# One group of small matmuls per pair of attention blocks instead of two: V of the 16 keys beyond 128, made for both blocks at once

## The reference

```python
win = xh.reshape(B, H // WS, WS, W // WS, WS, C).transpose(0, 1, 3, 2, 4, 5).reshape(-1, L, C)
qkv = (win @ qkv_w.T + qkv_b).reshape(-1, L, 3, HEADS, HD).transpose(2, 0, 3, 1, 4)
attn = jnp.einsum('bhld,bhmd->bhlm', q, k) * SCALE
attn = jax.nn.softmax(attn + bias[None], axis=-1)
out = jnp.einsum('bhlm,bhmd->bhld', attn, v).transpose(0, 2, 1, 3).reshape(-1, L, C)
out = out @ proj_w.T + proj_b
```

## Time and profile before

| | |
|---|---|
| median of 3 runs | 8950.28 us (8947.58 to 8953.78) |
| the profiled execution | 8950.57 us |
| its span | 8949.0 us |
| TensorE matmul busy (PE) | 8138.8 us, 91% |
| TensorE weight load busy (PEld) | 6102.6 us, 68% |
| VectorE (DVE), ScalarE (ACT), GpSimd (POOL) busy | 61%, 57%, 29% |
| mean granted clock of TensorE | 0.934 of full |

### The profile page before, as it was taken

How to read it: one execution, slowest core, us unless ns; L and a number is a source line. 1 busy time by engine, 2 the same in 40 slices (tenths; PEclk the granted TensorE clock), 3 DMA queues, 4 the chain that set the end, 5 groups by cost and what they waited for, 6 DMA issues and landing times.

```text
span 8949.0 us, 261096 instructions
## 1 busy us (share of the span) xinstructions
PE 8138.8 (91%) x88874; PEld 6102.6 (68%) x88874; DVE 5502.8 (61%) x20355; ACT 5135.3 (57%) x16576; POOL 2579.1 (29%) x3417
## 2 busy tenths in 40 slices
PE   9998999999999999999999999999999999999930
PEld 8996666866676667666686667666766667666720
DVE  4554777467845775377746784477637774678410
ACT  5554765466644664376546674466537653666434
POOL 1111333133322333133323332133313331334200
PEclk9998998999989998899999998999999999999865
DMA  7561000200012000200020000200020002000089
GB/s 125 97 110 35 15 21 21 82 12 21 15 32 69 21 21 15 86 15 21 22 76 18 21 15 24 77 21 21 15 86 15 21 22 84 10 21 15 23 329 410
DMA packets 386935, 487.38 MB, mean 54 GB/s; under 512 B 249617, under 2 KB 352529, under 8 KB 369297
## 3 DMA queue, kind: packets, MB, share of 16 engines
q1 hardware_dynamic: 369488, 393.67, 15.4%
q0 software_dynamic: 16192, 77.49, 2.2%
HBM read 319.45 MB, written 151.66 MB: 53 GB/s over the span
## 4 chain that ended last, share of the span: by engine, by line
PE 76%; issue 14%; DMA 4%; POOL 3%; DVE 2%; ACT 1%; POOLq 1%; SPq 0%; DVEq 0%; ACTq 0%
PE ps L946 66%; PE ps L1084 5%; POOL work L467 3%; DMA AH<-y_scratch 2%; PE ps L1129 2%; PE ps L1081 2%; DMA out<-AH 1%; PE ps L1082 1%; DVE work L801 1%; POOLq L464 0%; DVE work L765 0%; DVE work L811 0%; ACT AH L656 0%; ACT work L555 0%; POOL work L425 0%
## 5 line engine op out<-in xcount | busy, mean ns | idle before, releaser
L555 ACT ACTIVATE work<-work 128x144 f32<-128x144 f32 x5120 | 2042.8, 403 | 36.1 <-issue 35.1
L946 PE MATMUL ps<-work 128*32 128x144 f32 (+4 forms) x32902 | 1758.8, 302 | 160.0 <-issue 96.1
L765 DVE CUSTOM_DVE_ANT_0 work<-ps,negbias 128x144 f32<-128x144 f32 x5120 | 1247.1, 302 | 628.1 <-issue 435.2
L801 DVE SCALAR_TENSOR_TENSOR work<-xs,lw,work 128x570 f32<-128x570 f32 (+1 forms) x2048 | 1587.2, 812 | 0.0
L946 PEld LDWEIGHTS ps<-work 128*32 128x32 f32 (+3 forms) x32902 | 1009.9, 127 | 699.3 <-issue 563.1
L433 POOL TENSOR_TENSOR work<-work 128x80 f32<-128x80 f32 x1024 | 482.7, 471 | 3301.8 <-DVE work L772 3301.8
L946 PE MATMUL ps<-work,wqkv 128*128 128x288 f32 x4096 | 1319.4, 447 | 98.1 <-POOL work L448 78.9
L436 POOL TENSOR_TENSOR work<-work 128x640 f32<-128x640 f32 x1024 | 1309.1, 1278 | 0.0
L946 PEld LDWEIGHTS ps<-work,wqkv 128*128 128x128 f32 x4096 | 734.2, 197 | 382.9 <-POOL work L425 83.3
L555 ACT ACTIVATION_READ_ACCUMULATOR work<-work 128x1 f32 x5120 | 971.0, 190 | 0.0
L946 PE MATMUL ps<-wproj,work 128*96 128x256 f32 x3072 | 825.7, 393 | 0.0
(11 more groups left out here) (126 smaller groups left out, 11588.2 us busy)
## 6 DMA issues: line engine op xcount, KB each, us to landing
work<-in_x SPq DMA_DIRECT2D x128, 576.0 KB, 5.5
xs<-in_x SPq DMA_DIRECT2D x64, 1152.0 KB, 5.3
AH<-in_x SPq DMA_DIRECT2D x192, 384.0 KB, 3.4
y_scratch<-AH SPq DMA_DIRECT2D x192, 384.0 KB, 2.6
AH<-y_scratch SPq DMA_DIRECT2D x64, 1152.0 KB, 24.0
out<-AH POOLq DMA_DIRECT2D x64, 1152.0 KB, 17.0
xs<-in_x SPq DMA_DIRECT2D x112, 96.0 KB, 5.1
bias_scratch<-in_rpb_rev POOLq DMA_DIRECT2D x144, 4.5 KB, 2.1
```

Source lines behind the costliest of these rows:

```text
L555: o = act.activation(sp[t % 4][:, c, :], sp[t % 4][:, c, :], ACT.Exp, scale=-1.0, bias=mn[t % 4][:, c:c + 1], accum_out=den[t % 4][:, c:c ...
L765: v.tensor_tensor_reduce(out=sp[t % 4][:, c, :], in0=psS[c], in1=negbias[:, t % 2, c, :], scale=1.0, scalar=BIG, op0=ALU.add, op1=ALU.min, ...
L801: v.scalar_tensor_tensor(dst[:, ct, :, w0:w1], xs[side][:, ct, y0 + dy:y0 + dy + HS, w0 + dx - 1:w1 + dx - 1], lw[:, ct, tap:tap + 1], dst ...
L946: return nc.tensor.matmul(o, l, r, start=start, stop=stop)
```

## The change

Piece 5 loses its small matmuls. Piece 4's small matmuls take a stationary operand of 32 columns of x that holds the 16 pixels of block 0 and the 16 of block 1 (`xr`), which POOL copies together after the windows, behind a wait for its own window copies. V of the 16 keys then lies at partitions 32j to 32j+15 for block 0 and 32j+16 to 32j+31 for block 1, in one buffer for both blocks. `attend_few` contracts over all 32 rows; `normalise` writes the 16 keys' probabilities to columns 0 to 15 of `rest` for block 0 and to 16 to 31 for block 1, and the others stay zero from the memset at the head of an image (a buffer of `rest` always serves the same v). ScalarE's copy of piece 5 has 256 columns instead of 320. `xw_ready` is counted twice per pair.

```diff
-        v_sb = [carve("a", 2, C + CT * HD) for _ in range(2)]
+        xr = [carve("a", CT, 2, 16) for _ in range(2)]
+        v_sb = [carve("a", 2 * C + CT * HD) for _ in range(2)]
...
-                wait_apart(sy, (S["xw_ready"], n * NP - NP), (S["lpe_step"], n * 36 - 36))
+                wait_apart(sy, (S["xw_ready"], (n * NP - NP) * 2), (S["lpe_step"], n * 36 - 36))
...
                         last.then_inc(S["xw_ready"], 1)
+                        wait_apart(g, (S["xw_ready"], (n * NP + p) * 2 + 1))
+                        g.tensor_copy(xr[p % 2], xw[p % 2].rearrange("p t (v l) -> p t v l", v=2)[:, :, :, 0:16]
+                                      ).then_inc(S["xw_ready"], 1)
 
                     def normalise(t):
                         g.wait_ge(S["rden_ready"], n * NT + t + 1)
-                        g.tensor_tensor(rest[t % 4][:, :, 0:L - 128], sp[t % 4][:, :, 0:L - 128],
+                        v = t // 2 % 2
+                        g.tensor_tensor(rest[t % 4][:, :, 16 * v:16 * v + 16], sp[t % 4][:, :, 0:L - 128],
                                         rden[t % 4].unsqueeze(2).broadcast_to([128, LC, L - 128]),
...
-                            o = act.activation(v_sb[p % 2][:, k - 4], ps[:, psM, 0:C + CT * HD], ACT.Copy)
+                            n0, n1 = (0, C + CT * HD) if k == 4 else (C + CT * HD, 2 * C + CT * HD)
+                            o = act.activation(v_sb[p % 2][:, n0:n1], ps[:, psM, 0:n1 - n0], ACT.Copy)
...
-                            pe.wait_ge(S["xw_ready"], n * NP + p + 1)
+                            pe.wait_ge(S["xw_ready"], (n * NP + p + 1) * 2)
...
                             for kt in range(CT):
-                                mmul(ps[:, psM, 0:C], xp[:, kt, t0 + L - 128:t0 + L], wqkv[:, kt, 2 * C:3 * C],
-                                     start=kt == 0, stop=kt == CT - 1)
-                            for kt in range(CT):
+                                last = mmul(ps[:, psM, 0:C], xp[:, kt, t0 + L - 128:t0 + L], wqkv[:, kt, 2 * C:3 * C],
+                                            start=kt == 0, stop=kt == CT - 1)
+                            for kt in range(CT if k == 4 else 0):
                                 wv = wqkv[:, kt, 2 * C:3 * C].rearrange("p (g j d) -> p g j d", g=CT, j=HG)
                                 for j in range(HG):
-                                    last = mmul(ps[32 * j:32 * j + 32, psM, C:C + CT * HD], xp[:, kt, t0:t0 + 32],
+                                    last = mmul(ps[32 * j:32 * j + 32, psM, C:C + CT * HD], xr[p % 2][:, kt].rearrange("p v l -> p (v l)"),
                                                 wv[:, :, j, :], start=kt == 0, stop=kt == CT - 1)
...
-                            ch = 128 * hg + 32 * j
-                            mmul(psO[32 * j:32 * j + 32], v_sb[p % 2][:, v, ch:ch + 32], pt[t % 2][:, j, :],
+                            ch = (C + CT * HD) * v + 128 * hg + 32 * j
+                            mmul(psO[32 * j:32 * j + 32], v_sb[p % 2][:, ch:ch + 32], pt[t % 2][:, j, :],
                                  start=True, stop=False)
...
-                            few = slice(32 * j, 32 * j + L - 128)
-                            last = mmul(psO[32 * j:32 * j + 32], v_sb[p % 2][few, v, C + HD * hg:C + HD * hg + HD],
+                            few = slice(32 * j, 32 * j + 32)
+                            last = mmul(psO[32 * j:32 * j + 32], v_sb[p % 2][few, C + HD * hg:C + HD * hg + HD],
                                         pt[t % 2][few, HG, :], start=False, stop=True)
```

## The result

The changed kernel takes 8905.49 us (median of 8 runs, 8882.68 to 8928.03) against 8953.58 for the kernel before on the same chip (8 runs, 8947.58 to 8985.42). The ratio is 0.9943, 95% interval 0.9925 to 0.9961. So it is faster, by 48 us, where 76 were forecast, and 8905 lies outside the range of 8846 to 8898. Note the spread: 45 us over 8 runs of the changed kernel. The profiled execution took 8901.16 us, its span is 8899.5.

What follows compares the result with a forecast made beforehand. TensorE, 91% busy, was taken to bound the kernel. Terms -81.8 - 4 + 7 + 3 = -76 us against the profiled 8950.57 gave 8875, forecast as 8874 us against the median, 0.8% faster; range 8846 to 8898.

Steps and rivals of the forecast that it cites:

- Removed work: Piece 5's 16 small matmul records go, so attend starts 0.33 us earlier in 248 pairs: 81.8 us less (74.4 to 101.7).
- rival 1: Attend can't start earlier, its queue waits having been hidden beneath the small records: 12 us gain, about 8942 us; chance 6%.
- rival 2: Next wait, the fourth bank's or the end of the strips, takes back half the gain: 8915 us; chance 7%.
- attend_few over 32 rows: Contracting over 32 rows instead of 16 in attend_few takes 285 ns a record as before: costed at nothing.
- POOL at the heads: At each image's head POOL's two added copies and waits have no cover, 0.45 us each: +7 us (2 to 15).
- First pairs: In each image's first pair, ScalarE's copy behind piece 5 and then piece 6 come earlier: 4 us less (2.5 to 9).
- the end of the last strip: VectorE is nearly full there, so shorter TensorE steps only wait for it: 0 to 8 us lost, 3 taken.
- unkind end: Slowest total: removed work at 0.30 us a pair and all small terms at their unfavourable bounds, given as 8898 us.
- Rival 3: Slower by the clock: new gaps in the 64 strips drop TensorE to half clock, 1.7 us each: 8970 us; chance 3%.
- the granted clock would fall below 0.93: One of the signs in the changed profile that would show the prediction wrong.

Runs made afterwards that it cites:

- three copies: Changed kernel with table load moved and seam filled, POOL's copy to `xr` and its wait done three times instead of once: 8792.89 us, ratio 0.9819.

## Why the prediction was wrong

- **Removed work: right.** 0.33 us a pair was taken, 0.32 read off the two timelines; the attention stages give 82 us in the first pair of traces. Over all pairs of an image, with the half clock taken out at any price from 0.30 to 0.48, the start of piece 5 gains 0.34 to 0.36 us a pair in five traces of the changed kernel and 0.34 to 0.35 with the small matmuls alone left out. 248 x 0.35 = 87 where 82 stood. The worry of rival 1 (attend can't start earlier) did not come true, and rival 2's next wait neither.
- **attend_few over 32 rows: right** at nothing, 285 ns a record.
- **POOL at the heads: right**, 6 us against 7. The copy is 0.24 us there, its wait about 0.13, against 0.45 taken for both. In ordinary steps they take 0.7 us and are hidden, and three copies are.
- **First pairs and the end of the last strip** (-4 and +3). Not told apart: read from the traces, each changes with the price that is taken for the half clock. With the half clock taken out, the whole is 84 to 92 us where the terms gave 76; so the terms were too careful by about 12, of which 5 are the removed work's. (The sum's unkind end is 8897 by its own terms, not 8898, which changes nothing.)
- **What failed is the sum.** It subtracted the terms from the profiled execution's time as if all the rest stayed: a change of the half clock in the rest was put at nothing. The rest did not stay: the changed kernel's first trace has 859 us at half clock in the images against 780, and at 0.43 to 0.48 that is 34 to 38 us back of the 85 to 89 that the change is worth there. What is left is 51 us in the images, and 49.5 in the spans (8949.0 - 8899.5). Over all runs it is 91 us more at half clock, 39 us back of 86. That one execution of the changed kernel hit the forecast (8875.99) was luck: its images had 797 us at half clock, as before, and not 859.
- **Rival 3 had the right resource and the wrong place.** It priced the half clock nearly rightly (1.7 us lost in 3.4, where the images give 0.43 us for each), but looked for new idle time in the 64 strips. No new gap came: TensorE is idle in the attention stages for 5540.8 - 5257.6 = 283 us before and 5458.7 - 5173.7 = 285 after. The old ones, the table load and the seam, were there before the change, and how long the half clock lasts behind them varies with when they come. That the granted clock would fall below 0.93 stood among the signs of being wrong: it is 0.929.
- **The range** took in bounds of the terms alone. Three runs of the kernel before, 6 us apart, hid that the same program moves by more: by 45 us in the 17 runs beside the first experiments (8936.31 to 8981.54), by 43 and 19 beside the others.

TensorE: Matmul & The Clock Gate of the Trainium skill says under "HAM oscillation — how this bites in real kernels" that idle gaps between bursts of matmuls throttle the engine again. The traces agree with the direction: without the gaps of 1.6 and 1.2 us the half clock in the transform stages went from 175 to 270 us down to 12 to 14.

## What to carry to other kernels

Cut both spans into stages before adding up a change, and put the mean granted clock beside each: a local gain can be whole and still arrive by half, because stages that nobody touched run longer at the lower clock level. Where TensorE bounds a kernel, short idle places at seams (a table load, a last row that another engine still writes) are worth more than their length: 1.3 us and 1.2 us an image, taken away or filled, gave some 100 us on the changed kernel (ratio 0.9943 to 0.9829; the medians, on two chips, 8905 and 8793). And a comparison of two kernels whose clock is unsteady measures both; steady it first, or take the half clock's time off (0.43 us for each us here) and say how much that leaves unsure.

## What the runs showed that was not expected

- A delay of 9 us in all, put where nothing worked, made the changed kernel about 20 us faster (ratio 0.9921 against 0.9943 and 0.9945); twice the delay did not.
- The transform stage, 146.0 us at full clock, came out in few lengths only: 146.0 to 146.6, 148.8, 150 to 152, 155, 157 to 160 and 164 to 166 us, with 0 to 45 us at half clock.
- Once down, the clock took up to 44 us to come back, though TensorE was busy 43.80 of 44.00 us there (3441 to 3485 in the changed kernel's first trace).
- 16 matmul records of 64 columns take 0.33 us, 21 ns each, closer than the 25 ns that TensorE: Matmul & The Clock Gate of the Trainium skill gives as the least in "Wait — 56ns, not 53.3ns?". In the trace of the kernel before they start in fours, 7 ns apart, one for each group of 32 columns of the array, and the fours start 56 to 80 ns apart.
